# Windowed attention: transposing the probabilities in two 64-row groups, with weigh split in two and the residual one window later

## The chip, the cores and the metric

The kernel runs on one core of a Trainium2 chip. The metric is the time on the device in microseconds (us); several runs are taken and the median is compared. Of the core's engines, PE (TensorE) multiplies matrices into PSUM, DVE (VectorE) and ACT (ScalarE) work on SBUF and PSUM, POOL (GpSimd) on SBUF only, and SP issues transfers. Each engine works through its own instructions in the order of the program and waits for others by semaphores.

## The reference

Four stages follow one another, each `x = x + stage(groupnorm(x))`, on x of 4 x 32 x 96 x 96 in f32: windowed attention, a deformable convolution, a Fourier stage and a convolution by 8x8 Fourier blocks. The change is in the first alone:

```python
qkv = jnp.einsum('bchw,oc->bohw', x, w_qkv)          # 32 channels, 4 heads of 8
q = q.reshape(B * nh * nw, BLOCK * BLOCK, C) * d ** (-0.5)   # blocks of 8x8 queries
k = _unfold_halo(k, nh, nw)                          # windows of 14x14 keys
v = _unfold_halo(v, nh, nw)
k = jnp.concatenate([kh + rel_h, kw + rel_w], axis=-1)
sim = jnp.einsum('bid,bjd->bij', q, k)               # 64 queries x 196 keys, a head
attn = jax.nn.softmax(sim, axis=-1)
out = jnp.einsum('bij,bjd->bid', attn, v)
```

## The kernel before

The attention stage goes through 144 windows (12 rows of 12), each for all four batches at once. `w` is the window. The four batches are two pairs: `p` = 0 is batches 0 and 1, `p` = 1 is 2 and 3; `j` = 0, 1 is a pair of heads, so that two heads of 64 queries fill 128 partitions; `c` = 0, 1 is a half of the 196 keys (98 each). For one window:

- POOL makes the keys with their position terms (`keys`, L335) and the queries masked by head (`spread`, L329), for window w + 3.
- PE computes the scores of a pair (`scores`, L436): four calls, two batches in two row groups of 32 partitions and two PSUM banks, into `sc[p]`.
- DVE takes the negated maxima (`maxes`, L358), ACT the exponentials with their sums (`exps`, L412, four per pair) into `probs`, DVE the reciprocals of the sums (`inverse`, L363), POOL the product (`norm`, L340).
- PE transposes the probabilities (`transposed`, L447), for each batch four calls: 128 queries on the partitions become 98 keys on the partitions and 128 queries in the columns. A batch fills one PSUM bank, `pt[b % 2]`.
- The bank of an even batch is copied to `pts` by DVE (`evac`, L368), that of an odd one by ACT (`evac`, L404).
- PE weighs the values (`weigh`, L459): for both halves of the keys and each of the four batches a matmul into 32 partitions of `ov`, in four column groups, accumulating over c.
- DVE adds each head's part to `x_sb` (`residual`, L379): four operations, each waiting for the one before.
- SP loads the values two windows ahead (L311), as soon as `pv_done` of an older window allows it.

The order on each engine is written out by hand in its `step`. One step on PE: eight transposes of pair 0 of window w, scores of pair 0 of w + 2, weigh of w - 1, eight transposes of pair 1 of w, scores of pair 1 of w + 2. On DVE: evac 0, maxima of pair 0 of w + 2, reciprocals of pair 1 of w + 1, residual of w - 1, evac 2, reciprocals and maxima for w + 2. On ACT: exponentials of pair 1 of w + 1, evac 1, exponentials of pair 0 of w + 2, evac 3. On POOL: product of pair 0 of w + 1, keys, product of pair 1, queries. Each set of buffers is double; `pt` is two banks, so the transposes of a batch wait until the bank's last batch is copied out: even batches for DVE (`even_ready`), odd ones for ACT (`odd_ready`). Scores wait until the exponentials of the window before have read the bank. A wait stands in the engine's stream at the place where it is written and holds all that is behind it.

Of the kernel before, what the change touches and what calls it, by code (L numbers as in the profile page):

```python
# [137 lines left out]
def stage_attention(nc, x_dram, x_sb, wqkvT, rel, halves, headmask, ident_d, q_dram, v_dram):  # L138
# [4 lines left out]
    with ExitStack() as outer:  # L143
# [108 lines left out]
        with ExitStack() as ctx:  # L252
# [10 lines left out]
            pts = [[sbc(f"pts{i}_{b}", [HK, 2, 2, P]) for b in range(B)] for i in range(2)]  # L263
# [13 lines left out]
            def rows(eng, step):  # L277
# [10 lines left out]
                step(NWIN, NROW - 1, NROW)  # L288

# [65 lines left out]
            def _(dve):  # L355
# [9 lines left out]
                def evac(w, b, s):  # L365
                    wait(dve, pt_ready, w, B, b + 1)
                    wait(dve, pv_done, w, 1, -1)
                    nc.vector.tensor_copy(pts[s][b][:, :, :, :],  # L368
                                          pt[b % 2][0:HK, :].rearrange("p (c j q) -> p c j q", c=2, j=2)).then_inc(even_ready, 1)
# [13 lines left out]
                def step(w, gy, x):  # L383
# [6 lines left out]
                    if there(w + (-1)):  # L390
                        residual(w + (-1), gy, x - 1)
                    if there(w):
                        evac(w, 2, x % 2)
# [6 lines left out]
            def _(act):  # L400
                def evac(w, b, s):
                    wait(act, pt_ready, w, B, b + 1)
                    wait(act, pv_done, w, 1, -1)
                    nc.scalar.copy(pts[s][b][:, :, :, :],  # L404
                                   pt[b % 2][0:HK, :].rearrange("p (c j q) -> p c j q", c=2, j=2)).then_inc(odd_ready, 1)

                def exps(w, p, s):
                    wait(act, max_ready, w, 2, p + 1)
                    wait(act, pt_ready, w, B, 2 * p + 2 - 2 * B)
# [5 lines left out]
                def step(w, gy, x):  # L415
                    if there(w + 1):
                        exps(w + 1, 1, (x + 1) % 2)
                    if there(w):
                        evac(w, 1, x % 2)
                    if there(w + 2):  # L420
                        exps(w + 2, 0, x % 2)
                    if there(w):
                        evac(w, 3, x % 2)
# [3 lines left out]
            def _(pe):  # L427
# [12 lines left out]
                def transposed(w, b, s):  # L440
                    p = b // 2
                    wait(pe, normed, w, 2, p + 1)
                    wait(pe, (even_ready, odd_ready)[b % 2], w, 2, p)
                    for c in range(2):
                        for j in range(2):
                            o = (2 * c + j) * P
                            mm = nc.tensor.transpose(pt[b % 2][0:HK, o:o + P], probs[s][p][:, b % 2, j, HK * c:HK * c + HK], ident[:, :])  # L447
                    mm.then_inc(pt_ready, 1)

                def weigh(w, g, i):  # L450

                    s = i % 2
                    wait(pe, even_ready, w, 2, 2)
                    wait(pe, odd_ready, w, 2, 2)
                    wait(pe, v_loaded[s], g, 16 * VSRING, 32 * (i // 2 + 1))
# [1710 lines left out]
```

## Time and profile before

| | |
|---|---|
| runs (3) | median 2139.73 us, 2133.81 to 2160.07 |
| profiled execution | 2127.27 us, span 2125.5 us |
| PE busy over the span | 1895.2 us (89%), clock 0.934 of full |
| DVE, ACT, POOL busy | 1278.3, 1128.9, 789.2 us |
| transposes L447 | 2304 matmuls, 311.1 us busy |
| scores L436 | 2304 matmuls, 272.1 us busy |
| weigh L459 | 2304 matmuls, 155.0 us busy |
| copies of the transposes | DVE L368 288 x 681 ns, ACT L404 288 x 598 ns |

Busy times are unions, so matmuls that overlap are counted once. The mean duration of a matmul holds its latency, and their ends are modelled; what a matmul costs is read from the distance between starts. The span covers all four stages and the shares of the page are means over them; the attention loop is read from its own stretch.

### The profile page before, as it was taken

What the parts mean: (1) busy time and instruction counts of PE and PEld (TensorE: products, weight loads), DVE (VectorE), ACT (ScalarE), POOL (GpSimd) and SP (SyncE); (2) the same over time, 40 slices, a digit from 0 to 9 for tenths busy, and PEclk for the clock granted to TensorE, in tenths of its full rate; (3) what the DMA queues carried; (4) which work ended last, traced back from release to release, by engine and by line L of the source; (5) the groups of instructions that cost most, each with busy time, mean ns of one, the idle gap of its engine ahead of it and who ended that gap; (6) DMA issues with size and microseconds to landing.
All of it is one profiled execution on the core that took longest, in us unless ns stands there. A gap on an engine that the chain in (4) does not pass through costs nothing. (4 is left out here: it accounts for less than half of the span.)

```text
span 2125.5 us, 58757 instructions
## 1 busy us (share of the span) xinstructions
PE 1895.2 (89%) x21269; PEld 1344.1 (63%) x21269; DVE 1278.3 (60%) x2688; ACT 1128.9 (53%) x3617; POOL 789.2 (37%) x743
## 2 busy tenths in 40 slices
PE   5599999999999998389999999596949999999998
PEld 3466666666666665145555556395827787778876
DVE  5178888888888888258878878642372222222222
ACT  2378888888888887357777778200211111111111
POOL 0077878878787876133323333000000011001100
PEclk9989999999999999589999999855879999999999
DMA  4400000000000000566666665240022111221110
GB/s 165 134 20 28 28 27 23 27 26 28 23 28 26 28 24 23 142 169 186 190 185 191 181 175 143 59 71 11 11 55 51 40 36 36 52 56 36 36 36 15
DMA packets 164173, 150.01 MB, mean 71 GB/s; under 512 B 60070, under 2 KB 151340, under 8 KB 163935
## 3 DMA queue, kind: packets, MB, share of 16 engines
q1 hardware_dynamic: 164014, 147.88, 26.2%
q8 instruction: 101, 1.65, 0.3%
q14 instruction: 58, 0.47, 0.1%
HBM read 83.18 MB, written 45.89 MB: 61 GB/s over the span
## 5 line engine op out<-in xcount | busy, mean ns | idle before, releaser
L412 ACT ACTIVATE at_probs<-at_sc,at_nmx 128x196 f32<-128x196 f32 x1152 | 473.0, 423 | 114.2 <-DVE at_nmx L358 114.2
L340 POOL TENSOR_TENSOR at_probs<-at_probs,at_rs 128x784 f32<-128x784 f32 x288 | 429.9, 1493 | 152.9 <-DVE at_rs L363 152.8
L358 DVE TENSOR_REDUCE at_nmx<-at_sc 128x4 f32<-128x784 f32 x288 | 277.4, 963 | 122.3 <-PE at_sc L436 122.3
L447 PE MATMUL at_pt<-at_ident,at_probs 128*98 128x128 f32 x2304 | 311.1, 278 | 40.6 <-DVE at_pts L368 40.0
L447 PEld LDWEIGHTS at_pt<-at_ident,at_probs 128*98 128x98 f32 x2304 | 241.1, 128 | 141.2 <-POOL at_probs L340 78.8
L436 PE MATMUL at_sc<-at_kw,at_qw 32*128 32x196 f32 x2304 | 272.1, 355 | 12.0 <-POOL at_qw L329 8.1
L1247 ACT ACTIVATE dn_mix<-dn_mps 128x432 f32<-128x432 f32 x384 | 182.3, 528 | 114.1 <-PE dn_mps L1142 110.6
L1930 POOL TENSOR_TENSOR fc_spo<-fc_prod 128x256 f32<-128x256 f32 x72 | 52.2, 725 | 502.6 <-DVE fc_prod L1974 502.6
L2031 PE MATMUL fc_qps<-fc_wk,fc_xs 99*128 99x128 f32 x1728 | 208.4, 278 | 31.3 <-DMA fc_xs<-in_ones 31.3
L412 ACT ACTIVATION_READ_ACCUMULATOR at_probs<-at_sc,at_nmx 128x1 f32 x1152 | 235.9, 205 | 0.0
L2031 PEld LDWEIGHTS fc_qps<-fc_wk,fc_xs 99*128 99x128 f32 x1728 | 202.0, 194 | 42.0 <-issue 39.1
L436 PEld LDWEIGHTS at_sc<-at_kw,at_qw 32*128 32x128 f32 x2304 | 184.3, 187 | 65.3 <-issue 54.7
L1335 DVE TENSOR_SCALAR dn_mix<-dn_mps 128x432 f32<-128x432 f32 x384 | 213.2, 596 | 18.7 <-PE dn_mps L1142 18.7
L368 DVE COPY at_pts<-at_pt 98x512 f32<-98x512 f32 x288 | 196.0, 681 | 0.8 <-PE at_pt L447 0.8
L1155 PEld LDWEIGHTS dn_sps<-dn_mix,dn_patch 128*32 128x32 f32 x6144 | 141.2, 110 | 74.5 <-issue 56.6
L379 DVE SCALAR_TENSOR_TENSOR x_sb<-at_ov,at_hm,x_sb 128x64 f32 (+1 forms) x576 | 163.3, 284 | 27.8 <-PE at_ov L459 2.8
L1142 PE MATMUL dn_mps<-dn_stack,dn_selw 42*128 42x432 f16 x768 | 175.4, 346 | 1.1 <-DVE dn_mix L1335 0.6
L404 ACT COPY at_pts<-at_pt 98x512 f32<-98x512 f32 x288 | 172.3, 598 | 4.5 <-PE at_pt L447 4.5
L1155 PE MATMUL dn_sps<-dn_mix,dn_patch 128*32 128x96 f32 x6144 | 166.7, 247 | 3.7 <-issue 1.8
L1949 ACT COPY fc_vsb<-fc_vps 128x384 f32<-128x384 f32 x48 | 23.0, 478 | 272.0 <-PE fc_vps L2040 272.0
L1943 ACT COPY fc_spec<-fc_fps 128x1024 f32<-128x1024 f32 x72 | 73.0, 1014 | 176.8 <-PE fc_fps L2051 176.8
L1342 DVE COPY dn_sampled<-dn_sps 128x432 f32<-128x432 f32 x192 | 116.5, 607 | 83.1 <-PE dn_sps L1157 75.8
(155 smaller groups left out, 2527.9 us busy)
## 6 DMA issues: line engine op xcount, KB each, us to landing
fc_xs<-fc_xp SPq DMA_DIRECT2D x144, 120.0 KB
dn_slab<-near_image SPq DMA_DIRECT2D x72, 200.0 KB, 4.2
at_vs<-attention_values SPq DMA_DIRECT2D x288, 49.0 KB
dn_offs<-near_maps SPq DMA_DIRECT2D x24, 486.0 KB
near_corners<-dn_split SPq DMA_DIRECT2D x24, 486.0 KB
dn_stack<-near_corners SPq DMA_DIRECT2D x24, 486.0 KB
dn_patch<-near_pixels SPq DMA_DIRECT2D x24, 384.0 KB
attention_values<-ap_vrow SPq DMA_DIRECT2D x21, 256.0 KB, 2.3
```

The source lines that it names most:

```text
L340: nc.gpsimd.tensor_tensor(probs[s][p][:, :, :, :], probs[s][p][:, :, :, :], rs[s][:, 2 * p:2 * p + 2, :].unsqueeze(3).broadcast_to([P, 2, ...
L358: nc.vector.tensor_reduce(nmx[s][:, 2 * p:2 * p + 2, :], sc[p][:, :, 0:2 * NK].rearrange("p b (j k) -> p b j k", j=2), AX.X, ALU.max, nega ...
L368: nc.vector.tensor_copy(pts[s][b][:, :, :, :], pt[b % 2][0:HK, :].rearrange("p (c j q) -> p c j q", c=2, j=2)).then_inc(even_ready, 1)
L404: nc.scalar.copy(pts[s][b][:, :, :, :], pt[b % 2][0:HK, :].rearrange("p (c j q) -> p c j q", c=2, j=2)).then_inc(odd_ready, 1)
L412: nc.scalar.activation(probs[s][p][:, b, j, :], sc[p][:, b, NK * j:NK * j + NK], ACT.Exp, bias=nmx[s][:, 2 * p + b, j:j + 1], accum_out=su ...
L436: mm = nc.tensor.matmul(sc[p][:, b, NK * j:NK * j + NK], qw[s][r, 2 * j:2 * j + 2, :], kw[s][r, :], start=True, stop=True)
L447: mm = nc.tensor.transpose(pt[b % 2][0:HK, o:o + P], probs[s][p][:, b % 2, j, HK * c:HK * c + HK], ident[:, :])
L1142: nc.tensor.matmul(mps[b][:, 0:COLS], selw[:, :], stack[t % 2][:, b, :, :, 4 * k:4 * k + 4], start=True, stop=True).then_inc(mix_done, 1)
L1155: nc.tensor.matmul(sps[C * g:C * g + C, 2 * PX * b:2 * PX * b + 2 * PX], patch[t % 2][:, k, C * b:C * b + C], fours[:, :, g, :], start=Tru ...
L1247: nc.scalar.activation(mix[s % 2][b][:, :], mps[b][:, 0:COLS], ACT.Relu).then_inc(mix_act, 1)
L1335: nc.vector.tensor_scalar(mix[s % 2][b][:, :], mps[b][:, 0:COLS], 0.0, None, ALU.max).then_inc(mix_dve, 1)
L2031: mm = nc.tensor.matmul(qps[m][:, P * b:P * b + P], rows(i, b, dy * W + P * j, P), wk[:, dy, 0:2 * HID], start=(dy == 0), stop=(dy == 2))
```

## The change

Four things are changed, all in the attention stage.

1. A call transposes 64 queries, not 128: the rows `r` of `probs` are partitions 0 to 63 (h = 0) or 64 to 127 (h = 1), and go to bank `pt[0]` or `pt[1]`. One phase is now 16 calls for both batches of a pair, h alternating. The eight transposes that it replaces had one bank per batch.
2. After a phase, DVE copies `pt[0]` and ACT `pt[1]`, both waiting for the same `pt_ready`; the output is interleaved in runs of 64 in `pts[s][p]`. Each engine still copies two banks per window. A transposing phase waits for both copies of the phase before.
3. `weigh` is called by halves c: c = 0 after the scores of pair 0, c = 1 at the end of the step. The waits of the next transposing phase (`may_transpose`) stand ahead of the last of its four calls (b = 3).
4. `pv_done` thus comes at the end of PE's step, and DVE's residual takes window w - 2 in place of w - 1; there is one step more at the end of DVE's, ACT's and POOL's rows.

```diff
--- before.py
+++ after.py
@@ -260,7 +260,7 @@
             sums = [sbc(f"sums{i}", [P, B, 2]) for i in range(2)]
             rs = [sbc(f"rs{i}", [P, B, 2]) for i in range(2)]
             probs = [[sbc(f"probs{i}_{p}", [P, 2, 2, NK]) for p in range(2)] for i in range(2)]
-            pts = [[sbc(f"pts{i}_{b}", [HK, 2, 2, P]) for b in range(B)] for i in range(2)]
+            pts = [[sbc(f"pts{i}_{p}", [HK, 2, 2, 2, 2, Q64]) for p in range(2)] for i in range(2)]
             sc = [ctx.enter_context(nc.psum_tensor(f"at_sc{p}", [P, 2, 512], F)) for p in range(2)]
             pt = [ctx.enter_context(nc.psum_tensor(f"at_pt{i}", [P, 512], F)) for i in range(2)]
             ov = [ctx.enter_context(nc.psum_tensor(f"at_ov{i}", [P, 512], F)) for i in range(2)]
@@ -286,6 +286,7 @@
                 for x in range(NROW):
                     step((NROW - 1) * NROW + x, NROW - 1, x)
                 step(NWIN, NROW - 1, NROW)
+                step(NWIN + 1, NROW - 1, NROW + 1)
 
             def corner(gy, x):
 
@@ -362,11 +363,11 @@
                     wait(dve, exp_done, w, 4 * 2, 4 * p + 4)
                     nc.vector.reciprocal(rs[s][:, 2 * p:2 * p + 2, :], sums[s][:, 2 * p:2 * p + 2, :]).then_inc(inv_ready, 1)
 
-                def evac(w, b, s):
-                    wait(dve, pt_ready, w, B, b + 1)
+                def evac(w, p, s):
+                    wait(dve, pt_ready, w, 2, p + 1)
                     wait(dve, pv_done, w, 1, -1)
-                    nc.vector.tensor_copy(pts[s][b][:, :, :, :],
-                                          pt[b % 2][0:HK, :].rearrange("p (c j q) -> p c j q", c=2, j=2)).then_inc(even_ready, 1)
+                    nc.vector.tensor_copy(pts[s][p][:, :, :, :, 0, :].rearrange("p b c j q -> p (b c j) q"),
+                                          pt[0][0:HK, :].rearrange("p (n q) -> p n q", q=Q64)).then_inc(even_ready, 1)
 
                 def residual(w, gy, x):
                     y0, x0 = corner(gy, x)
@@ -387,10 +388,10 @@
                         maxes(w + 2, 0, x % 2)
                     if there(w + 1):
                         inverse(w + 1, 1, (x + 1) % 2)
-                    if there(w + (-1)):
-                        residual(w + (-1), gy, x - 1)
+                    if there(w + (-2)):
+                        residual(w + (-2), gy, x - 2)
                     if there(w):
-                        evac(w, 2, x % 2)
+                        evac(w, 1, x % 2)
                     if there(w + 2):
                         inverse(w + 2, 0, x % 2)
                         maxes(w + 2, 1, x % 2)
@@ -398,15 +399,15 @@
 
             @block.scalar
             def _(act):
-                def evac(w, b, s):
-                    wait(act, pt_ready, w, B, b + 1)
+                def evac(w, p, s):
+                    wait(act, pt_ready, w, 2, p + 1)
                     wait(act, pv_done, w, 1, -1)
-                    nc.scalar.copy(pts[s][b][:, :, :, :],
-                                   pt[b % 2][0:HK, :].rearrange("p (c j q) -> p c j q", c=2, j=2)).then_inc(odd_ready, 1)
+                    nc.scalar.copy(pts[s][p][:, :, :, :, 1, :].rearrange("p b c j q -> p (b c j) q"),
+                                   pt[1][0:HK, :].rearrange("p (n q) -> p n q", q=Q64)).then_inc(odd_ready, 1)
 
                 def exps(w, p, s):
                     wait(act, max_ready, w, 2, p + 1)
-                    wait(act, pt_ready, w, B, 2 * p + 2 - 2 * B)
+                    wait(act, pt_ready, w, 2, p + 1 - 2 * 2)
                     for b in range(2):
                         for j in range(2):
                             nc.scalar.activation(probs[s][p][:, b, j, :], sc[p][:, b, NK * j:NK * j + NK], ACT.Exp,
@@ -416,11 +417,11 @@
                     if there(w + 1):
                         exps(w + 1, 1, (x + 1) % 2)
                     if there(w):
-                        evac(w, 1, x % 2)
+                        evac(w, 0, x % 2)
                     if there(w + 2):
                         exps(w + 2, 0, x % 2)
                     if there(w):
-                        evac(w, 3, x % 2)
+                        evac(w, 1, x % 2)
                 rows(act, step)
 
             @block.tensor
@@ -437,43 +438,54 @@
                                                   start=True, stop=True)
                     mm.then_inc(scores_ready, 1)
 
-                def transposed(w, b, s):
-                    p = b // 2
+                def may_transpose(w, p):
                     wait(pe, normed, w, 2, p + 1)
-                    wait(pe, (even_ready, odd_ready)[b % 2], w, 2, p)
-                    for c in range(2):
-                        for j in range(2):
-                            o = (2 * c + j) * P
-                            mm = nc.tensor.transpose(pt[b % 2][0:HK, o:o + P], probs[s][p][:, b % 2, j, HK * c:HK * c + HK], ident[:, :])
+                    wait(pe, even_ready, w, 2, p)
+                    wait(pe, odd_ready, w, 2, p)
+
+                def transposed(w, p, s):
+                    for b in range(2):
+                        for c in range(2):
+                            for j in range(2):
+                                for h in range(2):
+                                    o, r = Q64 * (4 * b + 2 * c + j), slice(Q64 * h, Q64 * h + Q64)
+                                    mm = nc.tensor.transpose(pt[h][0:HK, o:o + Q64], probs[s][p][r, b, j, HK * c:HK * c + HK], ident[r, r])
                     mm.then_inc(pt_ready, 1)
 
-                def weigh(w, g, i):
+                def weigh(w, g, i, c, following):
 
                     s = i % 2
-                    wait(pe, even_ready, w, 2, 2)
-                    wait(pe, odd_ready, w, 2, 2)
-                    wait(pe, v_loaded[s], g, 16 * VSRING, 32 * (i // 2 + 1))
-                    wait(pe, res_step, w, HEADS, -HEADS)
-                    for c in range(2):
-                        for b in range(B):
-                            mm = nc.tensor.matmul(ov[s][C * b:C * b + C, 0:256], vs[i % VSRING][:, c, C * b:C * b + C],
-                                                  pts[s][b][:, c, :, :], start=(c == 0), stop=(c == 1))
-                    mm.then_inc(pv_done, 1)
+                    if c == 0:
+                        wait(pe, even_ready, w, 2, 2)
+                        wait(pe, odd_ready, w, 2, 2)
+                        wait(pe, v_loaded[s], g, 16 * VSRING, 32 * (i // 2 + 1))
+                        wait(pe, res_step, w, HEADS, -HEADS)
+                    for b in range(B):
+                        if b == B - 1 and following is not None:
+                            may_transpose(*following)
+                        mm = nc.tensor.matmul(ov[s][C * b:C * b + C, 0:256], vs[i % VSRING][:, c, C * b:C * b + C],
+                                              pts[s][b // 2][:, b % 2, c, :, :, :].rearrange("p j h q -> p (j h q)"), start=(c == 0), stop=(c == 1))
+                    if c == 1:
+                        mm.then_inc(pv_done, 1)
 
                 def step(w, g, i):
                     s = i % 2
                     if there(w):
+                        if not there(w + (-2)):
+                            may_transpose(w, 0)
                         transposed(w, 0, s)
-                        transposed(w, 1, s)
                     if there(w + 2):
                         scores(w + 2, 0, s)
                     if there(w + (-1)):
-                        weigh(w + (-1), g, i - 1)
+                        weigh(w + (-1), g, i - 1, 0, (w, 1) if there(w) else None)
+                    elif there(w):
+                        may_transpose(w, 1)
                     if there(w):
-                        transposed(w, 2, s)
-                        transposed(w, 3, s)
+                        transposed(w, 1, s)
                     if there(w + 2):
                         scores(w + 2, 1, s)
+                    if there(w + (-1)):
+                        weigh(w + (-1), g, i - 1, 1, (w + 1, 0) if there(w + 1) else None)
                 for w in range(-2, 2 * VSRING):
                     step(w, w // VSRING, w % VSRING)
                 with pe.Fori(2, NWIN // VSRING - 1) as g:
```

## Rows read from the trace of the kernel before

**Rows 1.** One source line, the residual: count, ns min/median/max, first and last start.

```profile
...
L379 DVE SCALAR_TENSOR_TENSOR x_sb<-at_ov,at_hm,x_sb x576: 253/284/288, 121.2 to 844.6; 128x64 f32 x160, 128x64 f32<-128x64 f32 x32
...
```

**Rows 2.** Busy time per stretch of 100 us (each engine: us and instructions), clock, DMA.

```profile
...
core 0: us, PE busy (x) PEld busy (x) DVE busy (x) ACT busy (x) POOL busy (x), PEclk, DMA share, GB/s
...
400.00:500.00 100.00, 94.04 (x947) 65.57 (x936) 85.66 (x199) 85.34 (x354) 80.07 (x79) 1.00 0.10 28
...
```

**Rows 3.** Waits from 300 to 600 us: waiting line, releaser, us in total, times, longest.

```profile
...
POOL at_probs L340 <- DVE at_rs L363: 60.8, 60, 1.0
ACT at_probs L412 <- DVE at_nmx L358: 43.9, 59, 0.8
...
DVE at_nmx L358 <- PE at_sc L436: 32.9, 59, 0.6
...
PE at_pt L447 <- DVE at_pts L368: 17.6, 59, 0.3
...
```

**Rows 4.** Timeline 402 to 409 us: start, us, engine, line, idle before it.

```profile
...
403.57 0.42 ACT L412 ACTIVATE at_probs<-at_sc,at_nmx 128x196 f32<-128x196 f32 x1 [0.74 <-DVE at_nmx L358]
...
403.63 0.93 PE L436 MATMUL at_sc<-at_kw,at_qw 32*128 32x196 f32 x8
...
404.49 1.07 PE L459 MATMUL at_ov<-at_pts,at_vs 98*32 98x256 f32 x16
404.61 0.97 DVE L358 TENSOR_REDUCE at_nmx<-at_sc 128x4 f32<-128x784 f32 x1 [0.55 <-PE at_sc L436]
...
405.18 0.60 ACT L404 COPY at_pts<-at_pt 98x512 f32<-98x512 f32 x1
...
405.49 1.08 PE L447 MATMUL at_pt<-at_ident,at_probs 128*98 128x128 f32 x8
...
405.62 1.53 SPq L311 DMA_DIRECT2D at_vs<-attention_values  x2
...
405.74 1.24 DVE L379 SCALAR_TENSOR_TENSOR x_sb<-at_ov,at_hm,x_sb 128x64 f32 x4
...
406.50 0.93 PE L436 MATMUL at_sc<-at_kw,at_qw 32*128 32x196 f32 x8
...
406.90 0.68 DVE L368 COPY at_pts<-at_pt 98x512 f32<-98x512 f32 x1
...
407.31 0.60 ACT L404 COPY at_pts<-at_pt 98x512 f32<-98x512 f32 x1
...
407.58 0.95 DVE L358 TENSOR_REDUCE at_nmx<-at_sc 128x4 f32<-128x784 f32 x1
407.70 0.83 PEld L447 LDWEIGHTS at_pt<-at_ident,at_probs 128*98 128x98 f32 x8 [0.57 <-POOL at_probs L340]
407.73 1.05 PE L447 MATMUL at_pt<-at_ident,at_probs 128*98 128x128 f32 x8 [0.30 <-DVE at_pts L368]
...
408.65 0.42 ACT L412 ACTIVATE at_probs<-at_sc,at_nmx 128x196 f32<-128x196 f32 x1 [0.74 <-DVE at_nmx L358]
...
408.71 0.60 PE L436 MATMUL at_sc<-at_kw,at_qw 32*128 32x196 f32 x4
...
```

**Rows 5.** Timeline of PE alone, three short windows at one phase's start.

```profile
...
405.49 0.32 PE L447 MATMUL at_pt<-at_ident,at_probs 128*98 128x128 f32 x1
...
405.49 0.42 PE L447 MATMUL at_pt<-at_ident,at_probs 128*98 128x128 f32 x2
...
405.49 0.53 PE L447 MATMUL at_pt<-at_ident,at_probs 128*98 128x128 f32 x3
...
```

**Rows 6.** Instructions by line and form, whole span: busy us, mean ns, idle before.

```profile
...
L1155 PE MATMUL dn_sps<-dn_mix,dn_patch 128*32 128x96 f32 x6144 | 166.7, 247 | 3.7 <-issue 1.8 <-DVE dn_sampled L1342 1.0 <-DVE dn_mix L1335 0.9
L459 PE MATMUL at_ov<-at_pts,at_vs 98*32 98x256 f32 x2304 | 155.0, 387 | 1.0 <-DVE at_pts L368 1.0
...
```

**Rows 7.** One source line, ScalarE writing 384 elements in permuted order.

```profile
...
L204 ACT ACTIVATE ap_qrow<-ap_ps x24: 490/490/490, 26.8 to 54.1; 128x384 f32<-128x384 f32 x24
...
```

**Rows 8.** One source line, ScalarE copying 384 elements in plain order.

```profile
...
L1949 ACT COPY fc_vsb<-fc_vps x48: 478/478/479, 1603.2 to 2114.7; 128x384 f32<-128x384 f32 x48
...
```

## The prediction

> **What bounds the kernel now.** First, where the change acts. The residual line runs from 121.2 to 844.6 us [rows 1]: 723.4 us for 143 steps, 5.06 us a window, out of a span of 2125.5. Everything outside that loop is untouched. Second, the busy time of each engine in one hundred microseconds of it [rows 2]: PE 94.0, DVE 85.7, ACT 85.3, POOL 80.1, at clock 1.00 (the 2.4 GHz level). So PE looks like the bound, but 6% of it is idle, and four engines this near to full are tied together by waits. Third, the waits [rows 3]: once per window (59 or 60 times in 300 us) POOL waits 1.0 us for the reciprocal, ACT 0.74 for the maxima, DVE 0.55 for the scores, and PE 0.30 for DVE's evacuation. That every engine waits, PE too, says that a ring of dependences sets the period. The timeline gives the ring [rows 4]. PE's pitch from phase to phase: weigh 404.49 to 405.49, 1.00; eight transposes 405.49 to 406.50 and 407.70 to 408.71, 1.01 each; scores 403.63 to 404.49, 0.86.
>
> The DVE ring before: scores start 403.63, maxima 404.61 (0.98); residual 405.74, evacuation 406.90, PE free to load at 407.70 (3.09 from the maxima); transposes 1.01; scores again at 408.71. Sum 0.98 + 3.09 + 1.01 = 5.08, the period exactly.
>
> The ACT ring before: scores to maxima 0.98; start of maxima to start of the exponentials that waited for them, 407.58 to 408.65, 1.07; four exponentials 403.57 to 405.18, 1.61; ACT's evacuation 0.60; 0.12 until PE loads (as 407.58, where DVE's copy ends, to 407.70); then the second half of the eight transposes, which alone waits for ACT, 0.50. Sum 4.88 [rows 4]. It has 0.20 to spare.
>
> Own work without waits: PE 5.08 - 0.30 = 4.78; DVE 5.08 - 0.55 = 4.53; ACT 5.08 - 0.74 = 4.34; POOL 5.08 - 1.01 = 4.07.
>
> **The transposes.** Before, 8 per phase of 128 moving columns. While one, two and three of them have started the union of their times grows 0.32, 0.42, 0.53 [rows 5]: 0.11 each, so 8 x 0.11 = 0.87 (0.109 unrounded) and 0.14 for the first load and the change from one kind of phase to the next. After, 16 of 64 columns, in pairs on two row groups and two banks. I take the cost as proportional to columns, 0.055, and two side by side: 8 x 0.055 + 0.14 = 0.58 instead of 1.01. That pairs on different rows overlap is seen in the scores: 8 matmuls of 196 columns would take 8 x 0.11 x 196/128 = 1.34 one after another and fit into 0.86; here two row groups of 32 are used. No row shows transposes so. From below: 8 pairs with no overhead at all, 0.44. From above: each as dear as one of 128 columns and none overlapped, 16 x 0.11 + 0.14 = 1.90. Between lies no overlap at the column price, 16 x 0.055 + 0.14 = 1.02. I take 0.58, since scores are the nearest row.
>
> The issue of twice as many instructions is not what I fear: 6144 matmuls with their loads take 166.7 us of PE [rows 6], 27 ns each, half of 0.055. The Trainium skill says otherwise ("TensorE: Matmul & The Clock Gate", section "Wait — 56ns, not 53.3ns?"): with hardware decode off the sequencer spends about 62 ns on each MATMUL. By that a phase would be an estimated 16 x 0.062 + 0.14 = 1.13; this trace disagrees with it, by the 27 ns.
>
> **Weigh is split in two**, one half after each scores phase. Sixteen matmuls of 256 columns, four side by side: 4 x 0.22 = 0.87 and 0.13 for load and phase change, the 1.00 seen [rows 4]. A half is 0.44 + 0.13 = 0.57, two make 1.13: +0.13 on PE. PE's own work after: 2 x (0.58 + 0.86 + 0.57) = 4.02, against 4.78. This is the gain offered: 0.76 us a window.
>
> **The waits.** What matters is where PE waits. Both transposing phases now need both evacuations of the phase before, and that wait stands ahead of the last matmul of the weigh half (b = 3). Queued behind it on PE is everything: that matmul, the transposes, the scores. When it is released, that one matmul still has its two passes to run (1152 calls are 2304 instructions [rows 6]) on one column group, one after the other: 2 x 0.22 + 0.13 = 0.57, as long as the whole half, since the other three groups can't help. If the wait came early the price would be nil. It doesn't, by the rings:
>
> ACT ring after: 0.98 + 1.07 + 1.61 + 0.60 + 0.12 as before = 4.38, then 0.57 (last matmul) + 0.58 (all sixteen transposes, where 0.50 stood) = 5.53. DVE ring after: 0.98 + 3.09 + 0.57 + 0.58 = 5.22. The ACT ring runs twice per window, once through each pair of batches (the second by the maxima, exponentials and evacuation of the other pair, through the same kinds of phases), each turn advancing one window, so both give 5.53 and don't add. The order of work on ACT (exponentials before evacuation) is what makes it a ring: ACT's evacuation of a pair stands behind exponentials whose scores were computed after the previous transposes.
>
> **The rest.** Two evacuations per engine and window stay, 98x512 each; their output now goes in runs of 64 with gaps. A permuted ScalarE write of 128x384 takes 490 ns [rows 7], a plain one 478 [rows 8]: up to 0.01 to 0.02 per evacuation, 2 us in all, which I leave in the range. The residual moves a window back on DVE: same four operations, no DMA, and its cover is DVE's slack (4.53 of 5.53); needed, because the values it reads are now complete only at the end of PE's step. The slot of ov it frees is asked for a window later, so PE doesn't wait for it. The loads of values wait for pv_done, half a step later than before, with two to three windows in hand (over 10 us) and 1.53 us of issue [rows 4]: nothing. POOL's product is due a window before its transposes: nothing. One more step at the end: about 1 us.
>
> Sum: 5.53 - 5.08 = +0.45 a window, x 144 = +65 us; 2127.3 (the profiled execution) + 65 = 2192. The median of the runs is 12.5 above the profiled one; between the two I put 2196.
>
> **Rivals.** (a) *Forecast*, ACT ring with the last matmul behind the wait: 62%, its own range 2170 to 2225. (b) *Transposes don't overlap*: 1.02 for 0.58, 5.97 a window, 2127 + 128 = 2255; for it, no transpose in a 64-row group stands in the trace; against it, the scores. With dearer forms (up to 1.90, 6.85, 2382): 14%. The skill's 62 ns would fall here, an estimated 2271. (c) *Not slower*: the last matmul costs nothing, because the wait is over when PE reaches it, or what is behind it isn't held. Then the ACT ring is 4.38 + 0.58 = 4.96, -0.12 a window, 2110. The place is b = 3 of each weigh half; slower by over 2% (42.8 us, 0.30 a window) starts at 5.38, thus where that matmul costs over 0.42. Between 0 and 0.42 it ends within 2%. For it, no row shows a wait inside a weigh phase; against it, PE has 0.57 + 0.58 + 0.86 = 2.01 of work from one release to the next b = 3, and half a window of 5.53 is 2.77, so it arrives some 0.7 early and waits. 19%. (d) *Faster by over 2%*, that is under 4.78 a window: PE's 0.76 would have to come through, down to DVE's 4.53, 2048. Even with a free matmul the ring stands at 4.96, so transposes would also have to take under 0.40, below the 0.44 bound. 5% for what I have misread.
>
> **Chances.** About 2% is what a measurement here can tell from no change. Faster 0.05 (d), same 0.19 (c), slower 0.76 (a, b). The range reaches from the dearer part of (c), 2140, to (b) at 2265.
>
> **What would show it.** Residual's first to last start: 790 us instead of 723. Windows: PE busy down from 94% to near 4.02/5.53 plus the lone matmul's passes, under 90%; ACT at 4.34/5.53, 78%. In the timeline, scores and maxima at pitch 5.53; a transposing phase of 0.58; 0.57 from ACT's evacuation plus 0.12 to the transposes; PE's wait charged to ACT's at_pts (L404), ahead of at_ov. ACT waits for maxima about 1.2 us a window. The forecast is wrong if sixteen transposes take about 1.0, if matmul b = 3 is short, or if the ring runs through DVE.

## The result and the profile after

| | before | after |
|---|---|---|
| runs | 4, median 2140.18 us | 4, median 2429.62 us (2421.62 to 2442.15) |
| ratio after / before | | 1.145, 95% interval 1.138 to 1.153 |
| profiled span | 2125.5 us | 2428.1 us |
| mean granted clock | 0.934 | 0.735 |
| PE busy | 1895.2 us | 2233.3 us |

The kernel is 14.5% slower. A kernel on this core also has longer executions at a lower mean clock (the kernel before, on one chip, 2100.56 us at 0.946 and 2174.13 us at 0.914), so ratios and their intervals are taken over the undisturbed executions, medians over all of them, and single times within some 3% of each other are compared by their loops. The page after, its rows of PE and its clock in 40 slices:

```profile
...
PE   5699999999999999999389999998766799999999
...
PEclk9855555555555555555589998999877899999999
...
```

PE is 90% busy or more in slices 3 to 19, and over the same slices the granted clock is 0.5. Where the loop lies is told by the residual (duration min/median/max, first and last start):

```profile
...
L380 DVE SCALAR_TENSOR_TENSOR x_sb<-at_ov,at_hm,x_sb x576: 252/284/286, 127.7 to 1157.1; 128x64 f32 x160, 128x64 f32<-128x64 f32 x32
...
```

1157.1 - 127.7 = 1029.4 us, against 723.4 before [rows 1]: 306 more, and the whole span grew by 302.6. So the loop accounts for all of it. Busy times of one stretch of it (us and instructions per engine, clock):

```profile
...
400.00:500.00 100.00, 100.00 (x890) 61.40 (x882) 62.09 (x138) 60.50 (x248) 55.14 (x55) 0.50 0.06 18
...
```

Beside [rows 2]: PE from 94.04 to 100.00, DVE from 85.66 to 62.09, clock from 1.00 to 0.50, which is 1.2 GHz in place of 2.4. The waits from 300 to 600 us (line, releaser, us, times, longest):

```profile
...
POOL at_probs L341 <- DVE at_rs L364: 131.4, 41, 3.2
ACT at_probs L413 <- DVE at_nmx L359: 117.5, 82, 1.4
...
DVE at_nmx L359 <- PE at_sc L437: 63.5, 83, 0.9
DVE at_pts L369 <- PE at_pt L452: 44.5, 42, 1.1
...
```

No row of these 300 us has PE waiting for ACT or DVE; all three other engines wait, in the end for PE. The 0.30 us per window of PE [rows 3] are gone and DVE now waits 44.5 us for transposes. The timeline (start, us, engine, line; in brackets the idle time ahead):

```profile
...
501.51 1.08 PE L466 MATMUL at_ov<-at_pts,at_vs 98*32 98x256 f32 x8
502.53 1.09 PE L452 MATMUL at_pt<-at_ident,at_probs 64*98 64x64 f32 x16
...
503.55 1.68 PE L437 MATMUL at_sc<-at_kw,at_qw 32*128 32x196 f32 x8
...
505.15 1.08 PE L466 MATMUL at_ov<-at_pts,at_vs 98*32 98x256 f32 x8
...
506.17 1.09 PE L452 MATMUL at_pt<-at_ident,at_probs 64*98 64x64 f32 x16
...
```

PE goes from phase to phase without a gap: half of weigh 501.51 to 502.53, 1.02; sixteen transposes 502.53 to 503.55, 1.02; scores 503.55 to 505.15, 1.60. Twice 3.64 is 7.28 us a window, for 5.08 (over the whole loop, with its ends, 1029.4 / 143 = 7.20 for 5.06). Each phase takes nearly twice what I had worked out (0.57, 0.58, 0.86), which is what half the clock does to it.

The kernel before ran through the same state for a moment. Its PE alone, at the start of the loop:

```profile
...
108.75 1.94 PE L447 MATMUL at_pt<-at_ident,at_probs 128*98 128x128 f32 x8
110.62 1.68 PE L436 MATMUL at_sc<-at_kw,at_qw 32*128 32x196 f32 x8
...
119.19 1.93 PE L459 MATMUL at_ov<-at_pts,at_vs 98*32 98x256 f32 x16
121.05 1.94 PE L447 MATMUL at_pt<-at_ident,at_probs 128*98 128x128 f32 x8
122.93 0.97 PE L436 MATMUL at_sc<-at_kw,at_qw 32*128 32x196 f32 x8
123.83 1.08 PE L447 MATMUL at_pt<-at_ident,at_probs 128*98 128x128 f32 x8
...
```

Eight transposes 108.75 to 110.62, 1.87; weigh 119.19 to 121.05, 1.86; PE without a gap from 108.75 on. Then the clock rose, and scores take 0.90 from 122.93 on; soon it is the 0.86 and 1.01 of [rows 4]. The changed kernel comes into its loop the same way, at the low level, and never leaves it.

### The profile page after: what moved, and what is told of

Read it like the earlier page. It is cut to its first block and busy times, and to the rows that moved or that the text cites. A ratio compares the mean times of both kernels' runs of the same rounds, so it can differ in the third digit from the quotient of the medians.

```text
span 2428.1 us, 62954 instructions
## 1 busy us (share of the span) xinstructions
PE 2233.3 (92%) x23573; PEld 1482.8 (61%) x23573; DVE 1304.3 (54%) x2688; ACT 1139.3 (47%) x3617; POOL 789.2 (33%) x743
## 5 line engine op out<-in xcount | busy, mean ns | idle before, releaser
L437 PE MATMUL at_sc<-at_kw,at_qw 32*128 32x196 f32 x2304 | 480.9, 569 | 12.0 <-POOL at_qw L330 8.0
L452 PEld LDWEIGHTS at_pt<-at_ident,at_probs 64*98 64x98 f32 x4608 | 254.1, 195 | 233.3 <-issue 233.3
L437 PEld LDWEIGHTS at_sc<-at_kw,at_qw 32*128 32x128 f32 x2304 | 331.6, 318 | 53.1 <-POOL at_qw L330 8.2
L452 PE MATMUL at_pt<-at_ident,at_probs 64*98 64x64 f32 x4608 | 314.5, 313 | 0.9 <-ACT at_pts L405 0.9
L466 PE MATMUL at_ov<-at_pts,at_vs 98*32 98x256 f32 x2304 | 314.5, 634 | 0.4 <-ACT at_pts L405 0.4
L1154 PE MATMUL dn_mps<-dn_stack,dn_selw 42*128 42x432 f16 x768 | 180.5, 353 | 4.3 <-issue 3.0
```

What stands on the lines that cost most here:

```text
L437: mm = nc.tensor.matmul(sc[p][:, b, NK * j:NK * j + NK], qw[s][r, 2 * j:2 * j + 2, :], kw[s][r, :], start=True, stop=True)
L452: mm = nc.tensor.transpose(pt[h][0:HK, o:o + Q64], probs[s][p][r, b, j, HK * c:HK * c + HK], ident[r, r])
L466: mm = nc.tensor.matmul(ov[s][C * b:C * b + C, 0:256], vs[i % VSRING][:, c, C * b:C * b + C], pts[s][b // 2][:, b % 2, c, :, :, :].rearran ...
L1154: nc.tensor.matmul(mps[b][:, 0:COLS], selw[:, :], stack[t % 2][:, b, :, :, 4 * k:4 * k + 4], start=True, stop=True).then_inc(mix_done, 1)
```

## The experiments

Three theories for the clock: (1) the transposes as they are now, (2) the order, with a phase more and a wait inside one, (3) only the level at which the loop is entered. And besides: do the rings of the prediction hold where the clock is full (granted clock 1.00)? In the diffs and the views a line of dots stands for lines that aren't shown. Where a kernel is stated with one time, that is one execution, beside 2118.46 us for the kernel before on the same chip, unless it says otherwise.

### Everything but the transposes

```diff
                             for j in range(2):
-                                for h in range(2):
-                                    o, r = Q64 * (4 * b + 2 * c + j), slice(Q64 * h, Q64 * h + Q64)
-                                    mm = nc.tensor.transpose(pt[h][0:HK, o:o + Q64], probs[s][p][r, b, j, HK * c:HK * c + HK], ident[r, r])
+                                o = (2 * c + j) * P
+                                mm = nc.tensor.transpose(pt[b][0:HK, o:o + P], probs[s][p][:, b, j, HK * c:HK * c + HK], ident[:, :])
 ...
```

The two copies are changed to match: DVE copies the bank of batch b = 0, ACT that of b = 1, without gaps in the output.

> Everything of the change but the transposes: they are again of 128 queries, 8 per phase, one bank per batch; weigh is split, the waits stand ahead of b = 3, the residual comes a window later. Theory 1 (it is the 64-query transposes that leave the clock at 1.2 GHz): clock 1.00 in the loop, and the rings of the prediction with a transposing phase of 1.01 can be seen: 4.38 + 0.57 + 1.01 = 5.96 us a window, 2254 us. Theory 2 (it is the order: weigh in two halves, more changes of phase, the wait inside a phase): clock 0.50 all through, PE alone sets 2 x 1.87 + 2 x 1.61 + 2 x 1.02 = 9.0 us a window, about 2690 us. Theory 3 (it is only how the loop was entered) allows either.

2271.99 us. A stretch of the loop, and the timeline of one window:

```profile
...
400.00:500.00 100.00, 92.49 (x808) 57.21 (x802) 76.02 (x169) 73.90 (x302) 69.32 (x68) 1.00 0.07 21
...
```

```profile
...
500.07 0.93 PE L435 MATMUL at_sc<-at_kw,at_qw 32*128 32x196 f32 x8
...
501.26 0.60 ACT L404 COPY at_pts<-at_pt 98x512 f32<-98x512 f32 x1
...
501.97 0.14 PEld L463 LDWEIGHTS at_ov<-at_pts,at_vs 98*32 98x32 f32 x2 [0.89 <-issue]
502.00 0.59 PE L463 MATMUL at_ov<-at_pts,at_vs 98*32 98x256 f32 x2 [0.44 <-ACT at_pts L404]
...
502.52 1.08 PE L449 MATMUL at_pt<-at_ident,at_probs 128*98 128x128 f32 x8
...
506.03 0.93 PE L435 MATMUL at_sc<-at_kw,at_qw 32*128 32x196 f32 x8
...
```

The clock is 1.00, so theory 2 falls. The window is 5.96 us (scores of the second pair at 500.07 and 506.03), the 5.96 worked out; the residual's first and last start, 129.9 and 980.9 us, are 851.0 apart for 723.4 before, +128 as expected. The remaining 26 of the +154 lie outside the loop (what differs there is read at the run with the residual late). The row at 502.00 is the lone matmul: its two passes (x2) come after ACT's copy (501.26 + 0.60), 0.44 idle ahead of them, and the transposes start at 502.52, 0.55 after its load at 501.97. The clock was 0.50 at the start of this loop too, and rose only at 159 us (123 in the kernel before).

### The transposes only

```diff
-                    if there(w + (-2)):
-                        residual(w + (-2), gy, x - 2)
+                    if there(w + (-1)):
+                        residual(w + (-1), gy, x - 1)
 ...
                     wait(pe, odd_ready, w, 2, p)
+                    k, m = C if p == 0 else HK, P if p == 0 else C
+                    nc.tensor.matmul(pt[0][0:m, 0:4], ident[0:k, 0:m], ident[0:k, 0:4], start=True, stop=True)
 ...
-                        if b == B - 1 and following is not None:
-                            may_transpose(*following)
 ...
-                        weigh(w + (-1), g, i - 1, 0, (w, 1) if there(w) else None)
-                    elif there(w):
+                        weigh(w + (-1), g, i - 1, 0, None)
+                        weigh(w + (-1), g, i - 1, 1, None)
+                    if there(w):
                         may_transpose(w, 1)
 ...
```

As the changed kernel, but weigh is whole again and the residual takes w - 1; the waits of `may_transpose` stand at the start of the phase, ahead of a small matmul.

> Only the transposes and their evacuation are changed, in the order of the kernel before (weigh whole, residual of w - 1); the waits stand ahead of the phase, on a matmul of 4 columns, about 0.1 us. Theory 1 (the transposes): clock 0.50 in the loop, PE full, 2 x 1.03 + 2 x 1.61 + 1.87 and some 0.2 for the small matmuls, 7.3 us a window, about 2430 us. Theory 2 (the order): clock 1.00, ACT ring 4.38 + 0.1 + 0.58 = 5.06, about 2125 us, like the kernel before. Theory 3 allows either.

2397.85 us.

```profile
...
400.00:500.00 100.00, 100.00 (x952) 76.34 (x951) 63.63 (x140) 63.03 (x252) 57.20 (x56) 0.50 0.06 18
...
```

Clock 0.50, PE full, windows of 7.16 us. Theory 1 stands on both runs: with the transposes changed the clock is low in either order, with them unchanged it is full.

### The loop entered at the full clock

```diff
+                def burn(n, k=0):
+                    for _ in range(n):
+                        nc.tensor.matmul(ov[k][:, 0:5 * PADDED], ident[:, :], kp[:, 0:5, :], start=True, stop=True)
+                burn(16)
                 for w in range(-2, 2 * VSRING):
+                    if w in (-1, 0):
+                        burn(4)
                     step(w, w // VSRING, w % VSRING)
```

> The changed kernel with dense matmuls of 128 rows put into PE's gaps ahead of the loop (16 calls of 510 columns before the first scores, 4 in each of two steps of the run-in), some 15 to 30 us more, so that the loop is entered at 2.4 GHz. Theory 3 (the loop only stays at the level at which it is entered): clock 1.00 from there on, 5.53 us a window, about 2210 us. Theories 1 and 2 (the loop's own work lets the clock fall): it falls back to 0.50 and stays, 7.28 us a window, about 2445 us.

2453.3 us.

```profile
...
120.00:130.00 10.00, 7.61 (x68) 4.54 (x70) 4.57 (x10) 6.62 (x29) 6.41 (x7) 1.00 0.00 0
130.00:140.00 10.00, 10.00 (x92) 6.25 (x95) 4.53 (x8) 6.63 (x27) 5.84 (x6) 0.52 0.04 10
...
400.00:500.00 100.00, 100.00 (x882) 61.87 (x878) 62.35 (x139) 61.37 (x252) 55.09 (x56) 0.50 0.07 20
...
```

PE alone, just ahead of the fall:

```profile
...
129.88 0.65 PE L452 MATMUL at_pt<-at_ident,at_probs 64*98 64x64 f32 x16 [1.92 <-ACT at_pts L405]
...
```

The clock is 1.00 from 103 to 130 us, while the extra matmuls and the run-in go on, and 0.50 from then on, with PE full. So entering at the full clock isn't enough to keep it, which theory 3 needs. But the fall comes in the run-in, 5 us after the last extra matmul and just after PE stood idle for 1.92 us; whether the steady loop would have lost the clock by itself this run doesn't show. The half of the transposes, below, shows a steady loop losing it.

### Idle matmuls, two and one per window

```diff
                         wait(pe, res_step, w, HEADS, -HEADS)
+                        for _ in range(2):
+                            nc.tensor.matmul(ov[s][:, 256:512], ident[:, :], kp[:, 0:4, 0:64], start=True, stop=True)
```

The second kernel has `range(1)`.

> The changed kernel with two idle matmuls per window (128 rows, 256 columns, results unused) ahead of weigh's first half. If a little more dense work on PE is what the clock lacks, it is 1.00: PE's own work is then 4.02 + 0.87 = 4.89, the ring of the prediction 5.53 (the idle work lies in PE's wait), about 2195 to 2215 us. If not, 7.28 + 1.73 = 9.0 us a window, about 2690 us. The ring of the prediction falls if the clock is 1.00 and the window is not 5.5 us.

> As filler2, with one idle matmul call per window in place of two. It brackets how much dense work the clock lacks. If one is enough: clock 1.00 and again 5.53 us a window, since the idle work lies in PE's wait, so the same time as filler2, 2180 us. If not: clock 0.50, PE alone sets 7.28 + 0.9 = 8.2 us a window, about 2550 us.

Two calls: 2180.47 us, with more work the faster by 249 us than the changed kernel. One call: 2608.55 us (the kernel before on that chip: 2129.62, median of 11). First two, then one:

```profile
...
130.00:140.00 10.00, 10.00 (x133) 6.17 (x125) 7.02 (x15) 6.54 (x28) 7.22 (x8) 0.94 0.10 31
...
400.00:500.00 100.00, 100.00 (x1232) 63.23 (x1231) 82.00 (x184) 78.32 (x326) 74.22 (x73) 1.00 0.08 25
...
```

```profile
...
400.00:500.00 100.00, 100.00 (x786) 59.35 (x786) 53.37 (x117) 53.12 (x212) 48.18 (x49) 0.50 0.05 16
...
```

With two the clock rises at 131 us and stays at 1.00; with one it stays at 0.50. It isn't the chip: on the chip of the second, two calls (the next experiment) and doubled transposes had 1.00 as well. My expectation that one might do was wrong, and its price in the low state was 8.4 us a window for my 8.2. With two the window can be read at full clock:

```profile
...
501.12 0.93 PE L437 MATMUL at_sc<-at_kw,at_qw 32*128 32x196 f32 x8
...
502.10 0.97 DVE L359 TENSOR_REDUCE at_nmx<-at_sc 128x4 f32<-128x784 f32 x1
...
503.19 0.42 ACT L413 ACTIVATE at_probs<-at_sc,at_nmx 128x196 f32<-128x196 f32 x1 [1.20 <-DVE at_nmx L359]
...
504.80 0.60 ACT L405 COPY at_pts<-at_pt 98x512 f32<-98x512 f32 x1
...
505.51 0.14 PEld L468 LDWEIGHTS at_ov<-at_pts,at_vs 98*32 98x32 f32 x2 [0.20 <-issue]
...
506.07 0.66 PE L452 MATMUL at_pt<-at_ident,at_probs 64*98 64x64 f32 x16
...
506.65 0.60 PE L437 MATMUL at_sc<-at_kw,at_qw 32*128 32x196 f32 x4
...
```

Every term of the ACT ring is here. Scores to maxima 501.12 to 502.10, 0.98; to the exponentials 503.19, 1.09; to the evacuation 504.80, 1.61; its 0.60 and 0.11 more to the load of the lone matmul at 505.51; 0.56 to the transposes at 506.07; 0.58 to the next scores at 506.65. Sum 5.53, as predicted. The loop takes 783.2 us by the residual's first and last start (128.8 to 912.0), 60 more than before, for the predicted 65; the whole time is 2180.47 - 2118.46 = 62 more.

### The wait behind the half of weigh

```diff
                     wait(pe, odd_ready, w, 2, p)
+                    k, m = HK, C
+                    nc.tensor.matmul(pt[0][0:m, 0:4], ident[0:k, 0:m], ident[0:k, 0:4], start=True, stop=True)
 ...
-                        if b == B - 1 and following is not None:
-                            may_transpose(*following)
 ...
```

`step` calls `may_transpose` ahead of both transposing phases; the two idle calls stay.

> filler2 with the waits of a transposing phase moved from ahead of b = 3 to behind the weigh half, onto a matmul of 4 columns. Ring theory (b = 3 behind the wait costs 0.57, of which some 0.1 stays with the small matmul): the ring falls from 5.53 to 5.06 and PE's own work sets the window, 4.02 + 1.06 for the idle matmuls as filler2 shows them + 0.2 for the two small ones = 5.28; 36 us less than filler2, about 2145 us. Rival (the place of the wait costs nothing, 5.53 comes from somewhere else): 5.5 us a window, 2180 us.

2163.63 us, median of 4 (2130.83 to 2165.66), beside 2129.62 on a chip whose own runs of the kernel before spread from 2100.56 to 2174.13. The totals of the two calls are from different chips, and their difference says nothing; the window does:

```profile
...
500.89 0.64 PE L468 MATMUL at_ov<-at_pts,at_vs 98*32 98x256 f32 x8
...
501.47 0.65 PE L454 MATMUL at_pt<-at_ident,at_probs 64*98 64x64 f32 x16
...
505.00 1.13 PE L466 MATMUL at_ov<-at_kp,at_ident 128*128 128x256 f32 x4
...
```

Whole windows measure 5.18 us (idle matmuls at 499.82 and 505.00), for 5.53 with the wait ahead of b = 3; the ring theory expected 5.28, its rival 5.5. The half of weigh, the small matmul and the change to the transposes now take 0.58 together (500.89 to 501.47; 0.64 in the other half of the window), and PE goes from phase to phase without a wait: PE's own work sets the window. So the place of the wait was worth 0.35 us a window at full clock.

### Each pair of transposes made twice

```diff
-                for h in range(2):
+                for h in (0, 1, 0, 1):
```

> The changed kernel with every pair of 64-query transposes made twice, into the same place: as many moving columns per row group as before the change, in the changed form. If it is the form (64 rows, two groups) that leaves the clock low: 0.50, 2 x (1.88 + 1.61 + 1.02) = 9.0 us a window, about 2690 us. If it is that half of the transposing work is gone: clock 1.00, ring 4.38 + 0.57 + 1.02 = 5.97, about 2250 us, as with the 128-query transposes in all_but_transposes.

2281.95 us (2129.62 beside it).

```profile
...
400.00:500.00 100.00, 100.00 (x1621) 63.17 (x1621) 74.08 (x169) 74.09 (x303) 67.81 (x67) 1.00 0.08 23
...
```

```profile
...
501.71 1.10 PE L452 MATMUL at_pt<-at_ident,at_probs 64*98 64x64 f32 x32
502.74 0.93 PE L437 MATMUL at_sc<-at_kw,at_qw 32*128 32x196 f32 x8
...
508.71 0.93 PE L437 MATMUL at_sc<-at_kw,at_qw 32*128 32x196 f32 x8
...
```

Clock 1.00 with the same 64-row form. Work done twice for nothing makes the kernel 148 us faster than the changed one. Windows are 5.97 us (502.74 to 508.71), as worked out. Thirty-two transposes take 1.03 (501.71 to 502.74) where sixteen take 0.58: 0.056 for each pair more, as the prediction had taken.

The row of 400 to 500 us also has a trap. PE's own phases are 2 x (1.03 + 0.86 + 0.57) = 4.92 of the 5.97, so PE waits about 1 us a window, ahead of b = 3; yet the profile shows it 100% busy, as in the run with two idle calls. The wait stands inside a row of matmuls and isn't seen as idle time. It is the distance from phase to phase that tells a PE that waits from a slow one.

### Half of the transposes, in the order and form of before

```diff
-                    for c in range(2):
+                    for c in range(2 if isinstance(w, int) and w < 4 else 1):
```

> The kernel before, in its own order and with its own 128-query transposes, but from the fifth window on only those of the first half of the keys are made (c = 0, 4 per phase in place of 8); the other half of pts holds old values, so this part of the computation is left out. If the missing transposing work is what the clock lacks, whatever its form: 0.50 all through the loop, 2 x (0.85 + 0.17) + 2 x 1.61 + 1.87 = 7.1 us a window, about 2420 us, slower than the kernel before although it does less. Rival (the form with two row groups is what counts): clock 1.00, the ACT ring 4.88 - 0.2 = about 4.7 or the DVE ring 0.98 + 3.09 + 0.57 = 4.64, 60 us faster than before.

2436.93 us, beside 2133.44 (median of 11).

```profile
...
150.00:160.00 10.00, 8.64 (x86) 4.84 (x82) 8.88 (x21) 8.74 (x39) 8.34 (x9) 1.00 0.08 23
...
170.00:180.00 10.00, 10.00 (x64) 5.45 (x60) 6.09 (x16) 7.54 (x33) 6.19 (x7) 0.50 0.04 12
...
400.00:500.00 100.00, 100.00 (x563) 59.19 (x563) 62.42 (x141) 63.71 (x255) 57.96 (x57) 0.50 0.06 18
...
```

The clock rose ahead of 140 us and was 1.00 until 170, in steady windows of 4.95 us (5.08 before) with PE 86% busy; then it fell, the windows take 7.12 (expected 7.1), and PE, now full, doesn't bring it back. The kernel before leaves out nothing and is 300 us faster. So neither the row groups nor the order is to blame, but that this part of PE's work became smaller. That PE was idle for 14% doesn't tell the two apart by itself: the last kernel below (PE's order alone) keeps 1.00 through its whole loop with PE 88% busy.

### Two orders without the new transposes

The residual behind DVE's evacuation, to cut the DVE ring of the prediction:

```diff
+                    if there(w):
+                        evac(w, 2, x % 2)
                     if there(w + (-1)):
                         residual(w + (-1), gy, x - 1)
-                    if there(w):
-                        evac(w, 2, x % 2)
```

> The kernel before, with the residual of w - 1 put behind DVE's evacuation of batch 2 instead of ahead of it. By the rings the DVE ring of 5.08 is cut (the evacuation no longer waits for 1.16 us of residual) and the ACT ring of 4.88 or PE's own 4.78 sets the window: 0.20 to 0.25 less, 25 to 35 us, 1.2 to 1.6% faster. Rival (four engines this full give nothing back, or the longest ring is another): no change.

2161.57 us, median of 6, beside 2129.62: ratio 1.020, interval 1.012 to 1.027. It is slower, whether by over 2% is open, and it isn't faster as forecast. The weigh phases and the maxima:

```profile
...
402.19 1.07 PE L459 MATMUL at_ov<-at_pts,at_vs 98*32 98x256 f32 x16
...
404.48 1.24 DVE L379 SCALAR_TENSOR_TENSOR x_sb<-at_ov,at_hm,x_sb 128x64 f32 x4
...
405.71 0.95 DVE L358 TENSOR_REDUCE at_nmx<-at_sc 128x4 f32<-128x784 f32 x1
...
407.25 1.07 PE L459 MATMUL at_ov<-at_pts,at_vs 98*32 98x256 f32 x16
...
```

The maxima of the second pair (405.71) now stand behind the residual (404.48 to 405.7), and with them the exponentials. The next windows begin at 407.25, 412.65 and 417.70, so that 5.06, 5.40 and 5.05 follow one another; the loop as a whole, by the residual's first and last start (122.5 to 865.2), is at 5.19 per window, for 5.06. The second ring had the same engine in it, and I had checked the first only. That loop is 19 us longer.

The rest isn't in the loop, and the traces say where it is: in the clock of the three stages behind it, which no kernel here changes. From the last residual to the end of the span the thirteen traces take 1255 to 1315 us (this one 1297.5, the kernel before 1280.9), and of that they spend 186 to 314 us at clock 0.50 (291 and 250). Take off half of that time, as if PE set the pace in it, and all thirteen lie between 1151 and 1167; that is an estimate, no run holds the clock of these stages fixed. So two kernels that differ in their attention loop alone also differ by up to some 60 us in how long the later stages run at the low level, and the loop is the better measure of a change in it.

Then both rings, on all three engines, with the 128-query transposes:

```diff
+                    if there(w + 2):
+                        scores(w + 2, 0, s)
                     if there(w):
                         transposed(w, 0, s)
                         transposed(w, 1, s)
-                    if there(w + 2):
-                        scores(w + 2, 0, s)
 ...
```

On PE the other half of the step is changed likewise. DVE's order is maxima 0, evacuation 0, reciprocals, residual of w - 2, maxima 1, reciprocals, evacuation 2; POOL's is product 0, keys, queries, product 1. The second kernel has PE's order alone.

> The kernel before with 128-query transposes; on PE each scores phase goes ahead of its transposing phase, on DVE the maxima ahead of the evacuation and the residual comes a window later, on POOL the queries ahead of the second product. By the rings: scores no longer stand behind transposes that wait for ACT's evacuation, so the ring through scores is 0.98 + 1.07 + 1.61 + 0.12 = 3.8, and PE's own 4.78 (DVE 4.53) sets the window: 0.2 to 0.3 less, 30 to 43 us, 1.4 to 2% faster than before. Rival: another ring of about 5 takes over, as for the residual behind the evacuation; no change or slower. The clock, on the work of PE being the same: 1.00.

> Only PE's order as in scores_first, DVE and POOL as before. The maxima then stand behind an evacuation that waits for the transposes: ring scores 0.86, transposes to the first bank 0.69, evacuation 0.60, maxima to exponentials 1.07, exponentials 1.61, 0.12: 4.95 us a window, 2100 to 2130 us, between the kernel before and scores_first.

All three: 2093.43 us, median of 6 (2059.68 to 2125.74), beside 2133.44, median of 11: ratio 0.983, interval 0.966 to 1.000. PE's order alone: 2164.12, one run.

```profile
...
500.65 1.06 PE L447 MATMUL at_pt<-at_ident,at_probs 128*98 128x128 f32 x8
...
505.40 0.84 PE L447 MATMUL at_pt<-at_ident,at_probs 128*98 128x128 f32 x6
...
```

PE is full, and the window 4.75 us (500.65 to 505.40), for 5.08: 0.33 x 144 = 47 us, at clock 1.00. By whole times the gain isn't settled, since the interval reaches 1.000; the loop is 50 us shorter by the residual (126.9 to 799.8, 672.9 for 723.4). Here the forecast of the window held (4.78, PE's own work). PE's order alone gave windows of 5.5 us, not 4.95. A stretch of that loop, and one of its waits from 300 to 600 us:

```profile
...
400.00:500.00 100.00, 88.08 (x885) 60.92 (x883) 79.89 (x182) 80.86 (x331) 73.81 (x73) 1.00 0.08 24
...
```

```profile
...
PE at_sc L436 <- POOL at_qw L329: 36.6, 55, 0.7
...
```

Scores waited for exponentials and then, once a window, 0.66 us for POOL's queries, which the other two engines' orders had put late.

## Why the prediction was wrong

**The step that failed** stands at its beginning, in the reading of the busy times: "at clock 1.00 (the 2.4 GHz level)". I carried that level into the time after, while it follows from what PE does: in the changed kernel's loop it is 0.50, PE's own work takes 7.28 us a window where I had 4.02, and that, not the ACT ring of 5.53, sets the pace. Every phase of the sum was priced at 2.4 GHz, and no rival asked what the loop would be at 1.2. The pieces for that case were in the trace: the loop of before starts at clock 0.50, with transposes at 1.87 and weigh at 1.86, and the sum at that level, 2 x (1.02 + 1.61 + 1.01) = 7.28, gives (7.28 - 5.08) x 144 = +317 us; the profiled executions are 303 apart, the loops 306. What the trace of before could not say is that taking transposes away would keep the clock low; the direction of the risk was there (PE's dense work was to fall by 0.76 us a window), its size was not.

**The transposes**: 0.58 was right, 0.58 at full clock with two idle matmuls (filler2) and 1.02 at half. Pairs in two row groups do run side by side. Sixteen calls in 0.58 are 36 ns each. The 62 ns per MATMUL that the Trainium skill has for hardware decode off ("TensorE: Matmul & The Clock Gate", section "Wait — 56ns, not 53.3ns?") did not bind here, by those 36 ns.

**The lone matmul behind the wait**: 0.57 predicted, right, 0.55 at full clock in all_but_transposes and filler2, and, by its absence, in filler2_waits. **Weigh in two halves**, 0.57 each: no trace shows a half at full clock with neither a wait nor a small matmul in it; with the small matmul it takes 0.58 to 0.64 (filler2_waits), so a half costs no more than that, and 1.02 at half the clock.

**The ring**: 5.53 predicted, 5.53 read at full clock; 5.96 for wide transposes, 5.96 read; 5.97 for doubled ones, 5.97 read. In the changed kernel itself no ring acts, since PE at half speed needs 7.28.

**Copies with gaps in their output**: 686 ns for 681 on DVE, 596 for 598 on ACT, nothing. **Residual, loads, product**: nothing, as said; in no row of 300 to 600 us does PE wait for one of them.

**Rivals**: (a) was true of a kernel whose clock holds, (b) and (c) were not. That it ends slower was right, but in the changed kernel for another reason than the one given, and its amount was off by more than four (303 for 65). **The marks** that I gave did half of their work: PE busy was to fall under 90% and rose to 100%, and that sent me to the clock. But the mark itself was wrong. With two idle matmuls and with doubled transposes the ring sets the window, and PE shows 100% too. What does tell them apart is the clock column and the distance between phases, 1.02 for 0.58.

What stays open: why the clock is granted as it is. The runs bracket it for this loop (one idle call per window leaves it low, two raise it, and so do the transposes made twice), but they don't separate the length of the work, its columns and its rows.

## What to carry to other kernels

Before pricing a saving on TensorE, look at the granted clock of the stretch and ask what the loop costs at 1.2 GHz; a change that takes dense work off PE can cost more than it saves, and a full PE in the profile is a sign neither of a full clock nor of a PE that doesn't wait. Look for the ring of waits, add its terms from one timeline, and then check the ring through the other half of the loop and through every other engine before cutting the first. A wait ahead of the last of several matmuls that run side by side leaves that one to run alone, at the price of the whole group.

## What the runs showed of the hardware

- The granted clock fell from 1.00 to 0.50 in a loop that kept PE 86% busy (half_transposes, 150 to 170 us), and stayed at 1.00 for 780 us at PE 88% busy (scores_first_pe). It stayed at 0.50 for a millisecond at PE 100% busy (the changed kernel).
- In the stages that no kernel changes, the time at clock 0.50 differed from trace to trace, 186 to 314 us, and their length with it, 1255 to 1315 us.
- More work made the loop faster three times over: two idle calls, 2180 for 2430 us; doubled transposes, 2282; and the transposes that half_transposes leaves out.
- A phase of transposes in 64-row groups costs 0.58 for the 1.01 of one in full rows, at 2.4 GHz. The work itself is halved (a pair of 64 columns 0.056, a call of 128 columns 0.109); the rest, 0.13 to 0.14 by subtraction, is for load and phase change and stays.
- A semaphore wait ahead of the last of four matmuls that run side by side in column groups costs as much as the four: 0.55 from its load to the next phase (all_but_transposes).
